# Evicting y by halves, first loads on both queues, and last additions of 3, 2, 2 and 1 tiles in a planned macaron kernel

## The reference, cut to what matters

```python
x = x + 0.5 * ffn(layernorm(x))        # per sequence: 8 experts, the best 2
x = x + attn(layernorm(x))             # the mixer
x = x + 0.5 * ffn(layernorm(x))

# ffn: mean over the tokens -> router logits -> softmax -> the 2 best experts, weights w0 + w1 = 1
#   out = w0 * (gelu(z @ w1[e0] + b1[e0]) @ w2[e0] + b2[e0]) + the same for e1       (128 -> 512 -> 128)
# attn: rmsnorm, convolution over 4 tokens, silu, projection to dt, v and gate,
#   rotation of v, a decayed running sum over the tokens, mixing of the heads, gate, output projection
```

## Time and profile before

| what | value |
|---|---|
| time, median of 3 runs | 259.94 us (259.83 to 260.12) |
| the profiled execution: its time, its span | 259.85 us, 258.1 us |
| mean granted TensorE clock | 0.998 |
| PE busy | 250.5 us, 97% of the span |
| DVE, ACT, POOL busy | 211.5, 195.1, 83.0 us |
| instructions | 4609 |

### The profile page before, as it was taken

How to read it: one execution, slowest core, us unless ns; L and a number is a source line. 1 busy time by engine, 2 the same in 40 slices (tenths; PEclk the granted TensorE clock), 3 DMA queues, 4 the chain that set the end, 5 groups by cost and what they waited for, 6 DMA issues and landing times.

```text
span 258.1 us, 4609 instructions
## 1 busy us (share of the span) xinstructions
PE 250.5 (97%) x1540; PEld 217.1 (84%) x1540; DVE 211.5 (82%) x536; ACT 195.1 (76%) x236; POOL 83.0 (32%) x90
## 2 busy tenths in 40 slices
PE   7899999999999999999999999999999999999994
PEld 6879999998998979899979899888678687887893
DVE  4767587798589799999999999999999997675612
ACT  1354665866999877969848989999989957979550
POOL 4234307910029601886502947400306002000000
PEclk9999999999999999999999999999999999999999
DMA  6699759746000176520600700700006000570022
GB/s 188 190 280 317 114 128 333 186 192 242 27 0 1 22 113 214 57 28 22 247 0 0 85 0 0 247 0 0 0 11 238 0 0 3 169 228 10 3 81 83
DMA packets 21975, 26.18 MB, mean 101 GB/s; under 512 B 1280, under 2 KB 17152, under 8 KB 21952
## 3 DMA queue, kind: packets, MB, share of 16 engines
q1 hardware_dynamic: 15440, 22.46, 26.6%
q0 software_dynamic: 5280, 2.88, 9.3%
q10 hardware_dynamic: 1232, 0.55, 0.8%
HBM read 16.98 MB, written 6.29 MB: 90 GB/s over the span
## 4 chain that ended last, share of the span: by engine, by line
PE 90%; ACT 3%; DMA 2%; issue 2%; DVE 1%; SPq 0%; ACTq 0%
PE hid_ps L839 32%; PE y_ps L867 28%; PE y_ps L892 10%; PE aux_ps L978 5%; PE aux_ps L934 4%; PE aux_ps L1010 3%; PE aux_ps L999 3%; DMA xt<-x_dram 1%; PE hid_ps L911 1%; PE y_ps L911 1%; PE aux_ps L959 1%; ACT hid L633 1%; ACT late L723 1%; DMA m_tok<-wpack_dram 1%; PE y_ps L1022 1%
## 5 line engine op out<-in xcount | busy, mean ns | idle before, releaser
L839 PE MATMUL hid_ps<-z_hi,w_parts 128*128 128x512 f32 x256 | 83.9, 410 | 0.4 <-ACT w_parts L586 0.4
L867 PEld LDWEIGHTS y_ps<-w_sb,hid 128*128 128x128 f32 x640 | 77.1, 192 | 4.3 <-DMA w_sb<-wpack_dram 0.7
L867 PE MATMUL y_ps<-w_sb,hid 128*128 128x128 f32 x640 | 78.1, 275 | 0.3 <-ACT hid L633 0.3
L633 ACT ACTIVATE hid<-hid_ps,w_sb 128x1024 f32<-128x1024 f32 x56 | 61.8, 1109 | 16.7 <-PE hid_ps L839 16.4
L839 PEld LDWEIGHTS hid_ps<-z_hi,w_parts 128*128 128x128 f32 x256 | 45.2, 189 | 9.5 <-issue 1.4
L839 PE MATMUL hid_ps<-z_lo,w_parts 128*128 128x512 f32 x128 | 40.1, 394 | 0.0
L1217 DVE TENSOR_TENSOR hid_lo<-hid,hid_hi 128x1024 fp32r<-128x1024 f32 x19 | 22.9, 1220 | 7.8 <-ACT hid_hi L640 7.8
L839 PEld LDWEIGHTS hid_ps<-z_lo,w_parts 128*128 128x128 f32 x128 | 24.0, 188 | 5.6
L640 ACT ACTIVATE hid_hi<-hid 128x1024 fp32r<-128x1024 f32 x19 | 19.6, 1055 | 1.3 <-PE y_ps L892 1.2
L480 POOL TENSOR_SCALAR bias_tok<-w_sb,coef 128x128 f32<-128x128 f32 x10 | 7.2, 730 | 38.7 <-DMA w_sb<-wpack_dram 24.8
L1104 DVE TENSOR_SCALAR f_tok<-xt,f_mv,f_rstd 128x128 f32<-128x128 f32 x64 | 17.6, 353 | 2.0 <-POOL f_rstd L458 1.9
(11 more groups left out here) (149 smaller groups left out, 462.9 us busy)
## 6 DMA issues: line engine op xcount, KB each, us to landing
w_parts<-w_split SPq DMA_DIRECT2D x12, 512.0 KB, 4.0
w_split<-mix_tmp SPq DMA_DIRECT2D x8, 512.0 KB, 4.7
w_sb<-wpack_dram SPq DMA_DIRECT2D x9, 322.5 KB, 3.9
xt<-bias_tok POOLq DMA_DIRECT2D x5, 512.0 KB, 6.5
late<-wpack_dram SPq DMA_DIRECT2D x2, 1024.0 KB, 6.8
w_sb<-wpack_dram SPq DMA_DIRECT2D x6, 258.5 KB, 4.2
xt<-x_dram SPq DMA_DIRECT2D x3, 512.0 KB, 8.4
out_dram<-xt SPq DMA_DIRECT2D x3, 512.0 KB, 3.2
```

What stands on the lines that cost most here:

```text
L633: nc.scalar.activation(hid[:, slot % HBUF, :], hid_ps[:, slot % 2, :], ACT.Gelu, bias=bias).then_inc(hid_ready, 1)
L839: last = nc.tensor.matmul(hid_ps[:, slot % 2, cols], w, z[:, q % 2, cols], start=first, stop=end)
L867: last = nc.tensor.matmul(y_ps[:, cols], hid[:, slot % HBUF, cols], w_sb[:, q % 2, k, W2_AT + f * P:W2_AT + (f + 1) * P], start=t == 0 and ...
```

## The change

The change has four parts. (1) In passes 5, 6 and 7, `pass_out` evicts y in two halves of 512 tokens, each with its own `yt_ready`; the last slot of the pass (`last_turned(q)`) runs its steps half by half, so that the first half of y is whole early (new semaphore `y_half_up`), and `post` and the next pass's first `down` wait for one half at a time. Before, only pass 7 was evicted by halves. (2) The second of x[0]'s four pieces is issued by ACT and the third by SP; before, SP issued the first two and ACT the last two. (3) The tail's additions and stores go in pieces of 3, 2, 2 and 1 tiles where they went in four of 2, and ACT stores the first and third of them, SP the second and fourth. (4) Nearly all places of the table `AT` are new.

```diff
-    QUARTERS = 4
+    PIECES = ((0, 3), (3, 5), (5, 7), (7, 8))
...
+        def last_turned(q):
+            return TAIL[0] - 1 if q == PASSES - 1 else SLOTS * (q + 1) - 1
...
-        def store_quarter(engine, i):
-            tiles = slice(i * NT // QUARTERS, (i + 1) * NT // QUARTERS)
+        def store_piece(engine, i):
+            tiles = slice(*PIECES[i])
             engine.wait_ge(x_final, i + 1)
...
-            for i in range(2):
+            for i in (0, 2):
                 sp.dma_start(xt[:, 0, 2 * i:2 * i + 2, :], x0[:, 2 * i:2 * i + 2, :]).then_inc(x0_in[i], 16)
...
-            for i in range(2, 4):
+            for i in (1, 3):
                 act.dma_start(xt[:, 0, 2 * i:2 * i + 2, :], x0[:, 2 * i:2 * i + 2, :]).then_inc(x0_in[i], 16)
...
-                for i, cols in enumerate(parts_of(q, N)):
-                    act.wait_ge(hid_used, (SLOTS * (q + 1) if q < PASSES - 1 else TAIL[0]) + i)
+                for half in range(2):
+                    cols = slice(half * HALF, (half + 1) * HALF)
+                    if half:
+                        act.wait_ge(hid_used, last_turned(q) + 1)
+                    else:
+                        act.wait_ge(y_half_up, turned_passes(q + 1))
                     nc.scalar.activation(yt[:, cols], y_ps[:, cols], ACT.Identity,
...
-                for i, (wt, src, ready) in enumerate(terms):
-                    if ready:
+                steps = [(i, half) for i in range(len(terms)) for half in range(2)]
+                if slot == last_turned(q):
+                    steps = [(i, half) for half in range(2) for i in range(len(terms))]
+                for i, half in steps:
+                    wt, src, ready = terms[i]
+                    if ready and half == 0:
                         pe.wait_ge(ready, split_slots(slot))
...
-                pe.wait_ge(yt_ready, turned_passes(q + 1))
                 for half in range(2):
                     free(half)
-                    if q == PASSES - 1:
-                        pe.wait_ge(yt_ready, turned_passes(q + 1) + half)
+                    pe.wait_ge(yt_ready, 2 * turned_passes(q) + 1 + half)
```

More of the change, by code:

```diff
@@ L59 @@
-        "y_turn_y": {5: 2206, 6: 2426, 7: 2600},
+        "f_norm": {1: 249, 2: 429, 3: 809, 4: 1129, 5: 1509, 6: 1829, 7: 2166},
+        "f_route": {1: 289, 2: 569, 3: 869, 4: 1189, 5: 1549, 6: 1860, 7: 2186},
+        "m_norm": {0: 489, 1: 849, 2: 1209, 3: 1489},
+        "m_dt": {0: 649, 1: 1009, 2: 1349, 3: 1746},
+        "m_v": {0: 689, 1: 1049, 2: 1409, 3: 1786},
+        "m_gate": {0: 769, 1: 1169, 2: 1589, 3: 1926},
+        "m_heads": {0: 929, 1: 1309, 2: 1700, 3: 2046},
+        "m_out": {0: 949, 1: 1329, 2: 1726, 3: 2066},
@@ L60 @@
+        "y_turn_y": {5: 2246, 6: 2366, 7: 2600},
     },
     "dve": {
[L62 to L68 removed]
@@ L129 @@
+        "y_store": {4: 1702, 5: 2335, 6: 2465},
     },
@@ L435, in _ @@
                     load_experts(q)
-            for i in range(0, QUARTERS, 2):
-                store_quarter(sp, i)
-            sp.wait_ge(out_done, 16 * (B - 1 + QUARTERS))
+            for i in range(1, len(PIECES), 2):
+                store_piece(sp, i)
+            sp.wait_ge(out_done, 16 * (B - 1 + len(PIECES)))
         @block.gpsimd
@@ L798, in _ @@
                     mixer_gate(b)
-            for i in range(1, QUARTERS, 2):
-                store_quarter(act, i)
+            for i in range(0, len(PIECES), 2):
+                store_piece(act, i)
         @block.tensor
@@ L858, in down @@
                     pe.wait_ge(w2_in[0][0], 16)
-                if t == 0 and q and not in_tokens(q - 1):
-                    pe.wait_ge(yt_ready, turned_passes(q))
                 if in_tokens(q):
@@ L883, in down @@
                     terms = [(w2, hid[:, slot % HBUF, :], None)]
-                for i, (wt, src, ready) in enumerate(terms):
-                    if ready:
-                        pe.wait_ge(ready, split_slots(slot))
-                    for half in range(2):
-                        cols = slice(half * HALF, (half + 1) * HALF)
-                        end = i == len(terms) - 1
-                        if t == 0 and i == 0 and q and in_tokens(q - 1):
-                            pe.wait_ge(x_updated, 2 * q - 1 + half)
-                        last = nc.tensor.matmul(y_ps[:, cols], wt, src[:, cols], start=t == 0 and i == 0,
-                                                stop=slot + 1 in (SLOTS * (q + 1), TAIL[0]) and end)
-                        if slot == TAIL[0] - 1 and end and half == 0:
-                            last.then_inc(hid_used, 1)
+                steps = [(i, half) for i in range(len(terms)) for half in range(2)]
[4 more added lines that the diff above has]
+                    if ready and half == 0:
+                        pe.wait_ge(ready, split_slots(slot))
+                    cols = slice(half * HALF, (half + 1) * HALF)
+                    end = i == len(terms) - 1
+                    if t == 0 and i == 0 and q and in_tokens(q - 1):
+                        pe.wait_ge(x_updated, 2 * q - 1 + half)
+                    elif t == 0 and i == 0 and q:
+                        pe.wait_ge(yt_ready, 2 * turned_passes(q) - 1 + half)
+                    last = nc.tensor.matmul(y_ps[:, cols], wt, src[:, cols], start=t == 0 and i == 0,
+                                            stop=slot == last_turned(q) and end)
+                    if slot == last_turned(q) and end and half == 0:
+                        last.then_inc(y_half_up, 1)
                 last.then_inc(hid_used, 1)
             def down_tail():
-                pe.wait_ge(yt_ready, turned_passes(PASSES) + 1)
+                pe.wait_ge(yt_ready, 2 * turned_passes(PASSES))
                 pe.wait_ge(w2_scaled, scaled_passes(PASSES))
@@ L907, in down_tail @@
                     for i in range(NT):
-                        if slot == TAIL[0] and i == NT // 2:
+                        if slot == TAIL[0] and i == PIECES[2][0]:
                             pe.wait_ge(hid_ready, TAIL[1] + 1)
```

151 lines of the change are left out of this document (73 added, 78 removed), and 6 rows, old and new, of the table AT.

## The result

The kernel after takes 260.42 us (median of 20 runs, 259.83 to 261.01), the kernel before in the same measurement 259.97 us (20 runs): a ratio of 1.0015, 95% interval [1.0008, 1.0021]. It is 0.4 us slower. That is within the 0.2% which the prediction counts as no change, but the interval leaves out 1, and the likeliest outcome of the prediction was 0.7 us faster: the time lies inside the range given, on the other side. The profiled executions point the same way: 261.01 us with a span of 259.2, against 259.85 and 258.1.

What follows compares the result with a forecast made beforehand. PE was taken as the bound, busy 250.5 of 258.1 us, with little to win in the middle. Terms -0.3 - 0.44 - 0.2 - 0.1 + 0.33 = -0.71 us took 259.94 to 259.2 us; range 258.3 to 260.5.

Steps and rivals of the forecast that it cites:

- Part 2, first loads: Start: x[0]'s second piece lands sooner on ACT's queue, and the chain behind it keeps the gain; -0.3 us, bounds 0 and -0.3.
- Part 4, the first gelu: Start: gelu(0) runs ahead of split_rest(0), so the first down starts sooner; -0.44 us, bounds -0.48 and -0.33.
- Part 1, halves: Pass 6's eviction: post(6) needs only the first half of yt, so PE waits less; -0.2 us, bounds -0.2 and 0.
- Part 3, the end: Tail: first store goes out 0.34 us later and the end follows the transfers; +0.33 us, bounds +0.33 and -0.9.
- Part 4, down(43), and the middle: PE's wait at down(43): a second split and an earlier gelu(42) nearly cancel; -0.1 us, bounds -0.56 and +0.95.
- A: Rival: the start's lead turns into a PE wait in the middle, for DVE or ACT; 260.1 us, chance 0.2.
- B: Rival: the new order opens a gap in DVE's full stretch, some 1.7 us passed on to PE; 260.9 us, chance 0.17.

Runs made afterwards that it cites:

- e10: e9 with x[0] loaded in the old order (SP issues the first two pieces, ACT the last two): 259.12 us, 0.9985 of the kernel before.
- e9: e3 with 10 early constant matmuls instead of 13: 258.52 us, 0.9949 of the kernel before.
- e2: The kernel before (old code) with the new table AT: 261.2 us, 1.0049 of the kernel before.
- e1: The new code with the whole old table AT: 259.44 us, 0.9975 of the kernel before.
- e8: e3 with the tail in four pieces of two tiles again: 258.96 us, 0.9962 of the kernel before.
- e3: The kernel after with new table places only where old and new are both below 650, old ones elsewhere: 258.7 us, 0.9963 of the kernel before.
- e13: The kernel after with ACT's scaling of mixer 2 put back behind gelu(29): 261.06 us, 1.0038 of the kernel before.
- e5: The kernel after with DVE's rotation (m_sin 2) put back behind the clamp: 260.4 us, 1.002 of the kernel before.
- e11: The kernel after with the last convolution tap of mixers 2 and 3 on 16 of 1024 columns: 260.54 us, 1.0023 of the kernel before.
- e14: The kernel after with the logarithm of mixer 3's step size on 16 of 1024 columns: 260.08 us, 1.0007 of the kernel before.
- e4: The kernel after with 10 early constant matmuls instead of 13: 259.85 us, 0.9998 of the kernel before.

## Why the prediction was wrong

*Part 2, first loads.* Predicted -0.3 us, with the second statistics at 3.9: so it is in the profile after (-0.35 to `f_tok`), and e10 has 0.41. The one clause that failed is that the rest is a chain behind it: the constant matmuls are in PE's queue too, took anything from 4.5 to 5.9 us, and ate it in the profiled execution. With 10 of them it is there in full (e9 against e10). The rule of the Trainium skill that I had against it (DMA: Bandwidth & Descriptors, "Queues, rings and completion order": both queues run on the same 16 DMA engines) left a term of 0 open, but every profile with the new order shows the gain; the fourth piece didn't come late enough for DVE to wait. Where the gain comes from can be seen in the issues: SP takes 0.96 us for its two of x[0], from 0.74 on, so the second one goes out 0.48 us after the first.

*Part 4, the first gelu.* Right in mechanism, -0.28 us for -0.44. I let the `gelu` start 0.65 us after PE's last pair but one; it starts 0.80 after (13.48 to 14.28), 0.18 behind the end of that pair where I had 0.03. The work moved into DVE's queue cost nothing, as forecast: the scaling waited 1.8 us and no wait of PE followed.

*Part 1, halves.* Right in mechanism: -0.25 to -0.28 us between `up(58)` and `up(60)` in every kernel with the new code, for -0.2, which I had also called the bound. It is the eviction by halves that gives it and not the new place of `post(6)`: e2, with that place and the old code, wins 0.06 there, and e1, with the old place and the new code, 0.28. Timeline of PE after, which answers to the earlier trace rows; `post(6)` starts 0.46 us behind the last pair of `up(58)`:

```profile
234.03 0.62 PE L850 MATMUL hid_ps<-z_hi,w_parts 128*128 128x512 f32 x2
234.49 1.03 PE L971 MATMUL aux_ps<-ident,yt 128*128 128x128 f32 x8
```

*Part 3, the end.* Predicted +0.33; it was 0 or a small gain. From PE's last matmul to the end of the span I had forecast 4.2 us; it is 3.55 to 3.66 us in all 16 profiles with the new pieces, and 3.87, 3.60 and 3.88 in the three with quarters (before, e2, e8). The first half of the argument held. Windows of the end of the kernel after, as the earlier trace rows, and the landing of its last four stores, as the earlier trace rows:

```profile
257.50:258.00 0.50, 0.00 (x0) 0.00 (x0) 0.00 (x0) 0.00 (x0) 0.00 (x0) 1.00 0.93 262
258.00:258.50 0.50, 0.00 (x0) 0.00 (x0) 0.00 (x0) 0.00 (x0) 0.00 (x0) 1.00 0.10 30
...
DMA to landing us min/median/max: 2.1/2.2/2.6
```

The DMA engines were full until about 257.97, which is 2.35 us behind PE's last matmul (255.62), where before it was 2.03 (254.23 to 256.26): the block does end 0.3 us later. What failed is the step from there to the end, that the last landing hangs on the end of the block: from the end of the block to the end of the span it is 1.2 to 1.3 us in all profiles with the pieces, and 1.84, 1.6 and 1.9 in the three with quarters. The last store, of 64 KB, landed 2.5 or 2.6 us after its issue in all 16, the one of 128 KB after 2.9, 2.6 and 2.9. Why the smaller one lands sooner behind a block that ends later, no run shows. The section of the Trainium skill that the prediction cites at this place is on transfers that GpSimd issues, while SP and ACT issue these; its estimate for the end, -0.1, came nearer all the same.

*Part 4, down(43), and the middle.* This is the step that failed. The prediction took PE's recorded waits for all that the middle holds ("a new order in the middle can win little more than that one wait"), followed that one wait, found its two changes cancelling (-0.1), and gave everything else between the first `down` and the end no term at all. The new order of the table from tick 650 on cost +1.4 us there. At `down(43)` the recorded wait is 0.81 instead of 0.56, inside the bounds that I gave, and by the starts of the slots 0.14 us are lost there. The other 1.3 us lie at `up(31)` (0.52), `up(39)` and `up(40)` (0.49) and `up(43)` (0.30), in gaps of 0.1 to 0.3 us that the list of waits doesn't show. That the order of the table is the cause is shown by e2 and e3; which places of it would have to go back isn't, beyond the 0.35 us of e13 and the 0.36 of e5. The forecast's own range, 258.8 to 259.6, was also too narrow by its own bounds: +0.95 at `down(43)` alone would have given 260.3.

*The rivals.* A, a lead from the start that is eaten in the middle, is refuted: with the old places in the middle the lead and the halves both reach the end, to 0.02 us (e3, e9), and with the new ones e2, which has next to no lead, loses as much as the kernel after. B is what happened, in another form. DVE does get new gaps in its full stretch, 0.90, 1.03 and 0.95 us between 90 and 112 us, and at 120 its `dstep` comes 2.0 us later than in e3, of which ACT waits 0.23 as shown above; but it isn't one wait of 1.7 us passed on whole, and DVE's work is not the price: less of it gave nothing (e11), less of ACT's gave a fifth (e14), and mending one place was lost again two slots on (e13, e5). I gave B a chance of 0.17 because the two places that I followed held. Of the table's 332 places 247 had moved, and two of them say little.

*The sum, with what was measured.* -0.35 (loads) - 0.28 (first gelu) - 0.27 (halves) + 1.40 (middle) + 0 (end) = +0.50 us, against +0.45 measured. That it comes so near is in part luck. It leaves out the constant matmuls, which eat part of the loads' gain (with 10 of them 0.4 us goes, e4) and cost the kernel before an amount that no run shows, and it leaves out up to 0.3 us that the end gained against two of the three profiles with quarters.

What stays open: why e13 is slower by 0.6 us than the kernel after, where the profiles differ by 0.1 (its eight runs go from 260.25 to 261.26, and the constant matmuls alone vary by 1.4 us), and the second group of e10's runs. A table that keeps the new middle and loses nothing wasn't found.

## What to carry to other kernels

Where three engines hand work to each other with 28 to 30 of 30 us busy, a list of waits says nothing about slack. Put an instruction of known length into each queue and see how much arrives (in the old order it was 0.74 of 1.21 us on DVE, 1.53 of 1.22 beside POOL, 0.92 of 0.96 on ACT), give a reordering there a term of its own with a loss in its range, and compare the starts of the slots one by one afterwards. A gain at the start or at the end of such a kernel can be had by itself: the new places of the start and the new code with the old middle are 0.5% faster than the kernel before, once the matmuls that only keep TensorE busy are fewer. And where a term says that the end follows the transfers, look at both parts in several profiles: here the block of transfers ended 0.3 us later, as counted, and the end of the span did not.
